# A vision-transformer tower on one core: two programs joined, weights split later, another order around the attention heads, and one exponential per tile

## The chip, the core and the metric

The kernel runs on one core of a Trainium2 chip. Five engines work side by side and meet through semaphores: TensorE (PE, matmuls; PEld is its weight load), VectorE (DVE), ScalarE (ACT), GpSimd (POOL) and SyncE (SP), which issues most transfers. Each engine takes its instructions in the order in which they are written. The metric is the time of one execution on the device in microseconds (us), lower is better; the profile is one execution, read by the hardware profiler.

## The reference, cut to what matters

64 images are cut into 36 patches each, embedded, and given two more tokens: 64 x 38 = 2432 tokens of 256 channels. Then comes an attention block (an mLSTM with four heads of 128 channels) and a feed-forward block with one shared expert and 32 routed ones, of which each token takes the best.

```python
h = embed(x) + positions                         # 64 x 38 tokens of 256
x_mlstm, z = split(layernorm(h) @ W_up)          # 2 x 512 channels
x_act = silu(causal_conv(x_mlstm, 4 taps))
q, k, v = headwise(x_act, Wq), headwise(x_act, Wk), headwise(x_mlstm, Wv)
ig, fg = concat(q, k, v) @ W_ig + b_ig, concat(q, k, v) @ W_fg + b_fg
logD = cumsum(log_sigmoid(fg))[s] - cumsum(log_sigmoid(fg))[t] + ig[t]     # for t <= s
mD = max over t of logD;  Dmat = exp(logD - mD)
C = q @ k.T * 128 ** -0.5 * Dmat
o = (C / max(|sum C|, exp(-mD))) @ v             # per image and head
state = (norm(o) * norm_w + skip * x_act) * silu(z)
h = h + state @ W_down
x2 = layernorm(h);  e = argmax(x2 @ gate_w);  s = sigmoid(max(x2 @ gate_w))
h = h + swiglu_shared(x2) + swiglu_e(x2 * s)     # expert e of 32, I = 512
```

## The kernel before, in words

The work has two parts, each a block of its own with one program per engine; at the end of the first block all engines meet before the second begins. `groups_phase` takes the images in eight groups of eight (304 tokens, four tiles of two images, 76 rows each). It is a software pipeline of eleven steps, written out by hand: `pipeline` calls `step(e, f, a, m)` on each engine, where `e` is the group that is embedded in this step, `f` the one before it (layer norm, up projection, convolution), `a` the one before that (attention), and `m` the oldest (feed-forward: router and shared expert). In five steps all four are there; the last step but two has no `e`, the last but one has only `a` and `m`, the last only `m`. The order of the calls in `step` is the order on that engine.

The names that matter: on PE, `decay` puts the exponent of the attention weights of one tile into a bank (a mask of -1e30, then per head a product of `pick` with `top_parts`, the negated running maximum of the gates), `heads` is the product of the weights with the values, `gate_up(m, k)` a quarter of the shared expert's two up products (12 matmuls), `ranks` counts tokens per expert, `shared_down` is the shared expert's second layer, `heads_t`, `down` and `att_rows` close the attention. On ACT, `decay(a, j)` takes the exponential of each of the four heads apart, since each has its own bias, a column of `a_gate`. On DVE, `weigh(a, j)` multiplies it with the scores, `expert_act(m, k)` multiplies the two halves of `gate_up(m, k)`, `rank_of` works on the counts, `head_stats`, `head_var`, `norm_2`, `last_channel` and `head_norm` normalise the heads. The banks of the heads are `ab` (2 to 5), those of the projections `fb` (0, 1), those of the feed-forward `mb` (6, 7).

Weights are kept in two parts (`_hi`, `_lo`), so that three fast products make one of nearly full precision. For the shared expert ACT and DVE split them (`split_shared`) in step 1, behind the first group's `f`; the last write of this preparation is `put_gate_columns`, and PE's first `q_of` waits for it (25 marks on `s_prep`).

`experts_phase` takes 32 slots of 128 tokens, one per expert, and up to 18 more for experts with more tokens. A slot: `x_of` (transposes), two `gate_up`, transposes of the product, `down`. Weights come in four buffers ahead. The rows of a slot were scattered by POOL in `xs_put` and `base_put` at the end of each group's `m`; `late_rows` finds the rows of tokens past 128, `count_slots` the extra slots. SP loads the first slot's rows when all 32 scatters (`s_x_put`) have landed.

Of the kernel before, what the change touches and what calls it, by code (L numbers as in the profile page):

```python
# [45 lines left out]
def groups_phase(nc, patches, w_lin, pos, cols, w_up, conv, chan, wq, wk, wv, wvt, w_gates, b_gates,  # L46
# [6 lines left out]
    with ExitStack() as ctx:  # L53
# [6 lines left out]

        ident = sort.ident
# [7 lines left out]
        up_hi = sb("up_hi", [128, KD, 2 * INNER], f32r)  # L69
        up_lo = sb("up_lo", [128, KD, 2 * INNER], f32r)  # L70
# [16 lines left out]
        pick = sb("pick", [AT, NT * NH, R], f32r)  # L87
# [11 lines left out]
        xn = sb("xn", [R, NT, D])  # L99
        xn_hi = sb("xn_hi", [128, KD, GT], f32r)  # L100
        xn_lo = sb("xn_lo", [128, KD, GT], f32r)
        xm = sb("xm", [128, 2, KI, GS, S])
        raw_vg = sb("raw_vg", [128, KI, GT])
        silu_z = sort.silu_z
        y = sb("y", [128, KI, GS, S])
        raw_qk = sb("raw_qk", [128, KI, GT])
        x_act = sort.x_act
        q_t = sb("q_t", [128, NH, NT, QW])
        c_t = sb("c_t", [R, NT, NH, QW])
        v = sb("v", [R, NT, INNER])  # L110
# [10 lines left out]
        top_parts = sb("top_parts", [AT, R], f32r)  # L121
        cw = sb("cw", [R, NT, NH, R])
# [103 lines left out]
        s_parts = sem("s_parts")  # L226
        s_top_mm = sem("s_top_mm")
# [64 lines left out]
        PREP_ALL = 25  # L292
# [18 lines left out]
        with nc.Block() as block:  # L311

            @block.sync
            def _(sp):
                sp.dma_start(lin_w[:], w_lin).then_inc(s_w_emb, 16)
# [7 lines left out]
                for dst, src in [(pos_t, pos), (col_t, cols)]:  # L323
                    sp.dma_start(dst[:], src).then_inc(s_w_emb, 16)
# [31 lines left out]
            def _(pool):  # L356
# [1599 lines left out]
```

## Time and profile before

| | |
|---|---|
| median of three runs | 744.8 us (743.41 to 746.59) |
| the profiled execution | 744.39 us |
| its span, first to last instruction | 742.6 us, mean granted PE clock 0.931 |
| PE busy | 657.5 us, 89% |
| DVE, ACT, POOL busy | 469.3, 390.6, 227.6 us |
| in the chain that ended last | PE 26%, issue 1%, DVE 1%, others 0% |

The profiled execution is 1.8 us longer than its span, and 0.4 us shorter than the median. The chain of waits reaches back only through the experts' part, so it says nothing of the groups; those are read from the timeline by engine. In a timeline row the first number is the start in us from the span's start, the second the time from the first start to the last end of the row's instructions, then engine, line and operation, and in brackets how long the engine sat idle before it and who ended that. Matmuls overlap, so the next row may begin before the row's end.

### The profile page before, as it was taken

The numbers are of one execution on the slowest core, as the hardware profiler recorded it, in microseconds if no ns is written. First come the engines' busy times: TensorE is split into PE (matmuls) and PEld (weight loads), VectorE is DVE, ScalarE is ACT, GpSimd is POOL, SyncE is SP. The second block draws the span as 40 slices with busy tenths as digits, with TensorE's granted clock in tenths as the row PEclk, the third lists the DMA queues.
The fourth block names the chain that finished last, engine by engine and source line by source line (L and its number), as shares of the span: only waits on it lengthen the run. The fifth ranks groups of instructions, "written<-read, shape, count | busy, mean of one in ns | idle before, by whom it ended". The sixth has DMA issues, their size and how long they took to land. (4 is left out here: it accounts for less than half of the span.)

```text
span 742.6 us, 11751 instructions
## 1 busy us (share of the span) xinstructions
PE 657.5 (89%) x4013; PEld 556.0 (75%) x4013; DVE 469.3 (63%) x1529; ACT 390.6 (53%) x856; POOL 227.6 (31%) x249
## 2 busy tenths in 40 slices
PE   4868999899999999899899978858599999999992
PEld 3757878878878878878878857737388888888782
DVE  1543666766766766766766763654567676767660
ACT  1335729629629629629629528302366666666660
POOL 3000011133033033133133133243356664312541
PEclk9698689999999999999999997977799999999997
DMA  8149010020020020020010010042599999999860
GB/s 307 64 124 359 24 49 1 18 83 18 18 82 19 18 82 19 18 81 19 19 33 20 18 32 16 18 137 102 174 369 379 378 380 375 322 409 345 292 241 15
DMA packets 46261, 101.69 MB, mean 137 GB/s; under 512 B 10952, under 2 KB 32246, under 8 KB 41329
## 3 DMA queue, kind: packets, MB, share of 16 engines
q1 hardware_dynamic: 35184, 89.07, 33.1%
q0 software_dynamic: 9488, 8.52, 4.4%
q10 hardware_dynamic: 1520, 3.23, 1.3%
q8 instruction: 37, 0.61, 0.3%
q14 instruction: 32, 0.25, 0.1%
HBM read 80.17 MB, written 23.32 MB: 139 GB/s over the span
## 5 line engine op out<-in xcount | busy, mean ns | idle before, releaser
L407 POOL TENSOR_TENSOR rstd_h<-var_h,minus_half 76x4 f32<-76x4 f32 x32 | 32.3, 1010 | 223.2 <-DVE var_h L844 223.2
L1671 POOL DMA_INDIRECT out<-rows,bg x32 | 37.5, 1171 | 72.0 <-DVE rows L1741 65.2
L1843 PE MATMUL bank<-w_hi,x_hi 128*128 128x512 f32 x148 | 57.6, 471 | 1.9 <-DVE x_lo L1753 1.9
L1075 PE MATMUL bank<-patch,lin_w 128*128 128x288 f32 x192 | 51.9, 424 | 7.8 <-DMA col_t<-cols 7.8
L451 ACT ACTIVATE att_t<-bank 128x304 f32<-128x304 f32 x16 | 6.8, 423 | 88.0 <-PE bank L1226 87.3
L1075 PEld LDWEIGHTS bank<-patch,lin_w 128*128 128x128 f32 x192 | 37.6, 200 | 18.2 <-POOL v L384 7.8
L748 DVE SCALAR_TENSOR_TENSOR y<-xm,conv_t,y 128x296 f32<-128x296 f32 (+2 forms) x96 | 44.3, 512 | 10.7 <-ACT xm L451 10.7
L1843 PE MATMUL bank<-w_lo,x_hi 128*128 128x512 f32 x148 | 47.0, 399 | 0.0
L1843 PE MATMUL bank<-w_hi,x_lo 128*128 128x512 f32 x148 | 46.6, 396 | 0.0
L1747 DVE TENSOR_TENSOR w_lo<-wts,w_hi 128x1024 fp32r<-128x1024 f32 x36 | 43.1, 1217 | 0.2 <-ACT w_hi L1794 0.2
L1466 POOL DMA_INDIRECT x_zone_dram<-xs_rows,spot x32 | 37.6, 1175 | 16.1 <-issue 8.9
L1466 POOL DMA_INDIRECT b_zone_dram<-base_rows,spot x32 | 37.1, 1160 | 16.5 <-issue 16.5
L1774 DVE TENSOR_TENSOR act_e<-silu_e,bank 128x512 f32<-128x512 f32 x37 | 25.5, 688 | 26.3 <-PE bank L1843 22.5
L1107 PE MATMUL bank<-xn_hi,up_hi 128*128 128x304 f32 x128 | 35.8, 364 | 5.6 <-DVE xn_lo L734 4.4
L1226 PE MATMUL bank<-hst,down_w 128*128 128x304 f32 x128 | 37.3, 448 | 3.5 <-DVE hst L864 3.5
L1107 PE MATMUL bank<-xn_hi,sgu_hi 128*128 128x304 f32 x128 | 33.5, 346 | 7.4 <-DVE logits L928 3.7
L1664 POOL DMA_INDIRECT listed_dram<-token,late_spot x32 | 36.3, 1134 | 9.8 <-issue 9.8
L1794 ACT ACTIVATE w_hi<-wts 128x1024 fp32r<-128x1024 f32 x36 | 37.0, 1050 | 1.9 <-DMA wts<-w_exp 1.9
L1818 ACT ACTIVATE silu_e<-bank 128x512 f32<-128x512 f32 x37 | 22.1, 596 | 28.8 <-PE bank L1843 28.0
L1741 DVE SCALAR_TENSOR_TENSOR rows<-bank,bg 128x256 f32<-128x256 f32 x37 | 15.7, 425 | 33.6 <-PE bank L1860 19.1
L1226 PEld LDWEIGHTS bank<-hst,down_w 128*128 128x128 f32 x128 | 26.1, 205 | 12.9 <-DVE hst L867 3.7
L1207 PE MATMUL bank<-v,cw 76*76 76x128 f32 x256 | 34.7, 296 | 1.0 <-DVE cw L798 1.0
(251 smaller groups left out, 1790.9 us busy)
## 6 DMA issues: line engine op xcount, KB each, us to landing
wts<-w_exp SPq DMA_DIRECT2D x18, 1024.0 KB
x_act<-w_exp SPq DMA_DIRECT2D x10, 1024.0 KB
silu_z<-w_exp SPq DMA_DIRECT2D x9, 1024.0 KB
wts_down<-w_exp SPq DMA_DIRECT2D x18, 512.0 KB
patch<-patches SPq DMA_DIRECT2D x8, 864.0 KB, 6.5
down_w<-w_exp SPq DMA_DIRECT2D x10, 512.0 KB
lin_w<-w_exp SPq DMA_DIRECT2D x9, 512.0 KB
b_zone_dram<-act_t SPq DMA_DIRECT2D x1, 4160.0 KB, 28.5
```

What stands on the lines that cost most here:

```text
L407: pool.tensor_tensor(rstd_h[:, j, :], var_h[:, j, :], minus_half[:], ALU.pow).then_inc(s_rstdh, 1)
L748: dve.scalar_tensor_tensor(y[:, k, :, lag:], xm[:, f.p, k, :, 0:S - lag], w, y[:, k, :, lag:], ALU.mult, ALU.add).then_inc(s_conv, 1)
L1075: last = pe.matmul(fb[c][:, 0:GS * N], lin_w[:, k, c * 128:(c + 1) * 128], patch[:, k, :], start=(k == 0), stop=(k == KF - 1))
L1107: last = pe.matmul(dst, weights[w][:, c, at:at + 128], x[part][:, c, :], start=(n == 0), stop=(n == 3 * KD - 1))
L1207: last = pe.matmul(ab[j][0:R, h * 128:(h + 1) * 128], cw[:, j, h, :], v[:, j, h * 128:(h + 1) * 128], start=True, stop=True)
L1226: last = pe.matmul(ab[c][:, 0:GT], down_w[:, k, c * 128:(c + 1) * 128], hst[:, k, :], start=(k == 0), stop=(k == KI - 1))
L1466: pool.indirect_dma_start(zone, bass.IndirectOffsetOnAxis(ap=self.spot[:, t:t + 1], axis=0), rows, None, bounds_check=E * SLOT - 1, oob_is ...
L1664: pool.indirect_dma_start(dram.listed, bass.IndirectOffsetOnAxis(ap=sort.late_spot[:, t:t + 1], axis=0), sort.token[:, t:t + 1], None, bou ...
L1671: pool.indirect_dma_start(out, bass.IndirectOffsetOnAxis(ap=rows_at, axis=0), rows[:, k % 4, :], None, bounds_check=T - 1, oob_is_err=Fals ...
L1747: dve.tensor_tensor(w_lo[:, k % 2, u, :], wts[k % 4][:, u * KD * I:(u + 1) * KD * I], w_hi[:, k % 2, u, :].bitcast(f32), ALU.subtract).the ...
L1794: act.activation(w_hi[:, k % 2, u, :], wts[k % 4][:, u * KD * I:(u + 1) * KD * I], ACT.Copy).then_inc(s_w_hi, 1)
L1843: last = pe.matmul(banks[2 + 2 * e + u][:, :], x[:, e, c * SLOT:(c + 1) * SLOT], w[:, e, u, c * I:(c + 1) * I], start=(n == 0), stop=(n == ...
```

## The change

The two blocks become one: the engines do not meet between the parts, and each walks from its last group into the experts. The last step of the pipeline is taken out of ACT's and DVE's `step` and written as `last_group`, called from the experts' first turn, with the first three splits of expert weights between its calls. SP's last stores are woven into the first loads of the experts' part. `late_rows` moves behind the second expert's product, and the experts use other banks. The shared weights have a buffer of their own and are split one step later; `put_gate_columns` goes into `merge_weights`, and `centre_values` before the embedding. On PE the last two `heads` come before `gate_up(m, 1)`, `up(f, 5)` goes between the heads, `up(f, 6)` before `ranks`, and the first of the four `q_of` products before `att_rows`. The gates no longer enter as ACT's bias: DVE makes `gate_parts`, PE adds them to the bank by one more product per tile, and ACT takes one exponential of 304 columns per tile.

The diff, without the change of indentation of both functions, cut to its core:

```diff
 (groups_phase, ACT)
 def decay(a, j):
 act.wait_ge(s_b_mm, NT * a.n + j + 1)
-for h in range(NH):
-g = NH * j + h
-act.activation(cw[:, j, h, :], ab[j][0:R, h * R:(h + 1) * R], ACT.Exp,
-bias=a_gate[:, g:g + 1]).then_inc(s_dmat, 1)
+act.activation(cw[:, j].rearrange("p h t -> p (h t)"), ab[j][0:R, 0:GT],
+ACT.Exp).then_inc(s_dmat, 1)
...
-if f and f.n == 0: split_shared()
+if f and f.n == 1: split_shared()
...
+def last_group(split):
+m = Group(G - 1, (G - 1) % 2)
+split(0, 0)
+xn2_t_of(m)
+split(0, 1)
+tanh_score(m)
+silu_g_of(m, 0)
+silu_g_of(m, 1)
+score_rows(m)
+silu_g_of(m, 2)
+split(1, 0)
+silu_g_of(m, 3)
+ffn_t_of(m)
 (groups_phase, DVE: merge_weights)
+dve.tensor_copy(q_t[:, :, :, R:], gx_w[:].unsqueeze(2).broadcast_to([128, NH, NT, 2 * NH])
+).then_inc(s_prep, 1)
 (top_gates)
+dve.tensor_scalar(gate_parts[:], ab[0][0:AT, 0:R], -1.0, None, ALU.mult).then_inc(s_gate_parts, 1)
...
+dve.wait_ge(s_gate_parts, 2 * a.n + 1)
+dve.scalar_tensor_tensor(gate_parts[LOW:, :], ab[0][LOW:AT, 0:R], -1.0,
+gate_parts[LOW:, :].bitcast(f32), ALU.mult,
+ALU.subtract).then_inc(s_gate_parts, 1)
 (step)
 weigh(a, 0)
 weigh(a, 1)
+weigh(a, 2)
+weigh(a, 3)
 if m:
 expert_act(m, 0)
 score_of(m)
-if a:
-weigh(a, 2)
-weigh(a, 3)
...
+def last_group(split):
+m = Group(G - 1, (G - 1) % 2)
+ln2_stats(m)
+xn2_of(m)
+split(0, 0)
+xn2_lo_of(m)
+route(m)
+choose(m)
+expert_act(m, 0)
+score_of(m)
+expert_act(m, 1)
+rank_of(m)
+split(0, 1)
+expert_act(m, 2)
+split(1, 0)
+expert_act(m, 3)
+dve.wait_ge(s_past, G)
+sort.count_slots(dve)
+base_of(m)
+sort.table_of(dve)
 (groups_phase, PE: decay)
 for h in range(NH):
-last = pe.matmul(ab[j][0:R, h * R:(h + 1) * R], pick[:, NH * j + h, :], top_parts[:],
-start=False, stop=(h == NH - 1))
+pe.matmul(ab[j][0:R, h * R:(h + 1) * R], pick[:, NH * j + h, :], top_parts[:],
+start=False, stop=False)
+last = pe.matmul(ab[j][0:R, 0:GT], gate_parts[:], pick[:, NH * j:NH * j + NH, :],
+start=False, stop=True)
 (step)
 heads(a, 0)
 heads(a, 1)
+if f: up(f, 5)
+if a:
+heads(a, 2)
+heads(a, 3)
+if m: gate_up(m, 1)
+if f:
+if f.n > 0: mixed_gates(f)
+up(f, 6)
 if m:
-gate_up(m, 1)
 ranks(m)
 gate_up(m, 2)
...
-if a:
-heads(a, 2)
-heads(a, 3)
-if f: up(f, 5)
 if m: gate_up(m, 3)
-if f:
-if f.n > 0: mixed_gates(f)
-up(f, 6)
-up(f, 7)
+if f: up(f, 7)
...
-if a:
-down(a)
-att_rows(a)
+if a: down(a)
+if f: q_of(f, range(0, 1))
+if a: att_rows(a)
 (experts_phase, SP)
+sort.last_rows(0)
+load_gate_up(2, sort.load, 2)
+sort.last_rows(1)
 sp.wait_ge(sort.s_x_put, 16 * TILES)
 load_x(0)
 load_x(1)
 (experts_phase, DVE: turn)
 if k == 0:
-w_lo_of(0, 0)
+sort.last_dve(w_lo_of)
 x_lo_of(k)
...
+if k == 1:
+sort.late_rows(dve)
```

PE in a full step, from the first heads to the counts. `v,cw` is `heads`, `xn2_hi,sgu_hi` and the two like it `gate_up`, `xn_hi,up_hi` and the two like it `up`, `hot` and `past` belong to `ranks`. Before:

```order
L1207 MATMUL bank2<-v,cw 76x128 x4
L1207 MATMUL bank3<-v,cw 76x128 x4
L1107 MATMUL bank6<-xn2_hi,sgu_hi 128x304 x2
L1107 MATMUL bank6<-xn2_hi,sgu_lo 128x304 x2
L1107 MATMUL bank6<-xn2_lo,sgu_hi 128x304 x2
L1107 MATMUL bank7<-xn2_hi,sgu_hi 128x304 x2
L1107 MATMUL bank7<-xn2_hi,sgu_lo 128x304 x2
L1107 MATMUL bank7<-xn2_lo,sgu_hi 128x304 x2
L1258 MATMUL bank7<-hot,before 76x128
```

In the changed kernel, from the same place:

```order
L1259 MATMUL bank2<-v,cw 76x128 x4
L1259 MATMUL bank3<-v,cw 76x128 x4
L1154 MATMUL bank1<-xn_hi,up_hi 128x304 x2
L1154 MATMUL bank1<-xn_hi,up_lo 128x304 x2
L1154 MATMUL bank1<-xn_lo,up_hi 128x304 x2
L1259 MATMUL bank4<-v,cw 76x128 x4
L1259 MATMUL bank5<-v,cw 76x128 x4
L1154 MATMUL bank6<-xn2_hi,sgu_hi 128x304 x2
L1154 MATMUL bank6<-xn2_hi,sgu_lo 128x304 x2
L1154 MATMUL bank6<-xn2_lo,sgu_hi 128x304 x2
L1154 MATMUL bank7<-xn2_hi,sgu_hi 128x304 x2
L1154 MATMUL bank7<-xn2_hi,sgu_lo 128x304 x2
```

The heads of the last two tiles and `up(f, 5)` (bank 1) now stand ahead of `gate_up(m, 1)` (banks 6 and 7); the counts stand further down, behind the gates' products and `up(f, 6)`.

DVE in the same step, from `weigh` (`cw`) to the first row of `rank_of` (`logits<-bank,hot`); `act_t` is `expert_act`, `y` the convolution. Before:

```order
L798 TENSOR_TENSOR cw<-c_t,cw 76x304 x2
L943 TENSOR_TENSOR act_t<-silu_g,bank 128x304
L921 TENSOR_SCALAR score<-tanh_s 76x4
L798 TENSOR_TENSOR cw<-c_t,cw 76x304 x2
L748 SCALAR_TENSOR_TENSOR y<-xm,conv_t,y 128x8x36 x2
L943 TENSOR_TENSOR act_t<-silu_g,bank 128x304
L748 SCALAR_TENSOR_TENSOR y<-xm,conv_t,y 128x8x35 x2
L748 SCALAR_TENSOR_TENSOR y<-xm,conv_t,y 128x8x37 x2
L928 TENSOR_TENSOR logits<-bank,hot 76x128
```

In the changed kernel:

```order
L826 TENSOR_TENSOR cw<-c_t,cw 76x304 x4
L971 TENSOR_TENSOR act_t<-silu_g,bank 128x304
L949 TENSOR_SCALAR score<-tanh_s 76x4
L771 SCALAR_TENSOR_TENSOR y<-xm,conv_t,y 128x8x36 x2
L971 TENSOR_TENSOR act_t<-silu_g,bank 128x304
L771 SCALAR_TENSOR_TENSOR y<-xm,conv_t,y 128x8x35 x2
L771 SCALAR_TENSOR_TENSOR y<-xm,conv_t,y 128x8x37 x2
L956 TENSOR_TENSOR logits<-bank,hot 76x128
```

All four `weigh` come first; between the first and the second `expert_act` one pair of the convolution is left, and everything behind the second stands behind it as before.

DVE at the seam, where the last group goes over into the experts: `base_rows` is the last group's, `o`, `late_f`, `early` and `late_spot` are `late_rows`, `x_lo` and `act_e` belong to the experts. Before:

```order
L950 TENSOR_TENSOR base_rows<-bank,h 76x2x256 x2
L1509 TENSOR_TENSOR o<-hot,start_row 76x1024
L1511 TENSOR_REDUCE late_f<-o 76x32
L1512 TENSOR_SCALAR early<-rank 76x32
L1513 TENSOR_TENSOR late_f<-late_f,rank 76x32
L1514 TENSOR_TENSOR late_spot<-late_f,early 76x32
L1516 CAST table<-bank 1x18
L1517 CAST table<-end_slot 1x1
L311 UNCONDITIONAL_BRANCH
L1734 UNCONDITIONAL_BRANCH
L1747 TENSOR_TENSOR w_lo<-x_act,w_hi 128x1024
L1753 TENSOR_TENSOR x_lo<-bank,x_hi 128x256
```

In the changed kernel, from the same `base_rows`:

```order
L978 TENSOR_TENSOR base_rows<-bank,h 76x2x256 x2
L1573 CAST table<-bank 1x18
L1574 CAST table<-end_slot 1x1
L1811 TENSOR_TENSOR x_lo<-bank,x_hi 128x256
L1835 TENSOR_TENSOR act_e<-silu_e,bank 128x512
L1811 TENSOR_TENSOR x_lo<-bank,x_hi 128x256
L1805 TENSOR_TENSOR w_lo<-silu_z,w_hi 128x1024
L1805 TENSOR_TENSOR w_lo<-wts,w_hi 128x1024
L1835 TENSOR_TENSOR act_e<-silu_e,bank 128x512
L1563 TENSOR_TENSOR o<-hot,start_row 76x1024
L1565 TENSOR_REDUCE late_f<-o 76x32
L1566 TENSOR_SCALAR early<-rank 76x32
```

`late_rows` has moved from before the first expert's `x_lo` to between the second expert's product and the third expert's `x_lo`.


## Rows read from the trace of the kernel before

**Rows 1.** the page: the granted clock of PE in 40 slices of the span, in tenths

```profile
PEclk9698689999999999999999997977799999999997
```

**Rows 2.** two steps of the loop: busy time by engine, granted clock (from:to, us, engines)

```profile
220.00:275.70 55.70, 52.94 (x373) 45.87 (x373) 39.40 (x163) 32.16 (x83) 16.11 (x17) 0.97 0.13 40
275.70:331.30 55.60, 51.83 (x374) 44.50 (x375) 39.31 (x163) 32.16 (x83) 16.12 (x17) 1.00 0.13 40
```

**Rows 3.** first and last `att_rows` of the full steps (start us, us, engine, line)

```profile
108.60 1.07 PE L1084 MATMUL bank<-ident,att_t 128*76 128x128 f32 x8 [0.51 <-ACT att_t L451]
386.90 1.07 PE L1084 MATMUL bank<-ident,att_t 128*76 128x128 f32 x8 [0.51 <-ACT att_t L451]
```

**Rows 4.** PE in one step, from the end of the decays; last, the step after

```profile
240.78 0.87 PE L1107 MATMUL bank<-xn_hi,up_hi 128*128 128x304 f32 x2
244.84 1.91 PE L1207 MATMUL bank<-v,cw 76*76 76x128 f32 x16
249.15 0.22 PE L1258 MATMUL bank<-hot,before 76*76 76x128 bf16 x1 [0.72 <-DVE act_t L943]
251.06 0.52 PE L1107 MATMUL bank<-xn_hi,sgu_hi 128*128 128x304 f32 x2 [0.61 <-DVE logits L928]
251.98 1.91 PE L1207 MATMUL bank<-v,cw 76*76 76x128 f32 x16
259.05 4.25 PE L1285 MATMUL bank<-act_t,sd_w 128*128 128x304 f32 x16
302.01 0.55 PE L1107 MATMUL bank<-xn_hi,sgu_hi 128*128 128x304 f32 x2 [1.03 <-ACT silu_g L580]
```

**Rows 5.** DVE in the same step: the experts' products and the last head channel

```profile
248.53 0.47 DVE L943 TENSOR_TENSOR act_t<-silu_g,bank 128x304 f32<-128x304 f32 x1
252.25 0.47 DVE L943 TENSOR_TENSOR act_t<-silu_g,bank 128x304 f32<-128x304 f32 x1
256.94 0.47 DVE L943 TENSOR_TENSOR act_t<-silu_g,bank 128x304 f32<-128x304 f32 x1
265.13 0.15 DVE L849 SCALAR_TENSOR_TENSOR o<-mv_h,rstd_h 76x4 f32<-76x4 f32 x1
```

**Rows 6.** ACT in the same step: the score copies and the 16 exponentials

```profile
224.79 2.19 ACT L451 ACTIVATE c_t<-bank 76x336 f32<-76x336 f32 x4
240.89 3.49 ACT L541 ACTIVATE cw<-bank,a_gate 76x76 f32<-76x76 f32 x16
```

**Rows 7.** PE in the step without an embedding, after waits

```profile
432.36 1.24 PE L1217 MATMUL bank<-ident,o 76*128 76x76 f32 x16 [0.54 <-DVE o L849]
435.36 5.92 PE L1226 MATMUL bank<-hst,down_w 128*128 128x304 f32 x16 [1.75 <-DVE hst L864]
```

**Rows 8.** PE and DVE at the end of the first group's preparation

```profile
57.00 4.39 PE L1133 MATMUL bank<-x_act,score_w 128*128 128x304 f32 x8 [5.52 <-DVE q_t L704]
54.10 1.22 DVE L661 TENSOR_TENSOR sgu_lo<-hst,sgu_hi 128x1024 fp32r<-128x1024 f32 x1
```

**Rows 9.** the seam: links of the chain of waits (start us, us, what)

```profile
526.55 2.02 DMA xg<-x_zone_dram
535.18 0.69 DVE act_e L1774
539.98 1.73 PE bank L1860 x8
```

**Rows 10.** the seam: PE's last transposes of the groups, first expert product

```profile
521.03 1.07 PE L1084 MATMUL bank<-ident,ffn_t 128*76 128x128 f32 x8 [0.29 <-ACT ffn_t L451]
530.23 1.22 PE L1843 MATMUL bank<-w_hi,x_hi 128*128 128x512 f32 x2 [0.93 <-DVE x_lo L1753]
```

**Rows 11.** the seam: the two long operations of `late_rows` on DVE

```profile
523.00 1.21 DVE L1509 TENSOR_TENSOR o<-hot,start_row 76x1024 f32<-76x1024 bf16 x1
524.25 1.22 DVE L1511 TENSOR_REDUCE late_f<-o 76x32 f32<-76x1024 f32 x1
```

**Rows 12.** the seam: POOL's last scatter of expert inputs

```profile
518.82 1.13 POOL L1466 DMA_INDIRECT x_zone_dram<-xs_rows,spot  x1 [0.30 <-issue]
```

More of the change, by code:

```diff
@@ L226, in groups_phase @@
         s_parts = sem("s_parts")
+        s_gate_parts = sem("s_gate_parts")
         s_top_mm = sem("s_top_mm")
@@ L1266, in gate_up @@
-                def gate_up(m, k):
-                    if k == 0:
-                        pe.wait_ge(s_lgt, m.n + 1)
-                        if m.n == 0:
-                            pe.wait_ge(s_prep, 23)
-                    else:
-                        pe.wait_ge(s_sg, KI * m.n + k)
-                    for u in range(2):
-                        if u and k:
-                            pe.wait_ge(s_act, KI * m.n + k)
-                        if u and k == 2:
-                            pe.wait_ge(s_own, m.n + 1)
-                        at = u * I + k * 128
-                        split_product(mb[u][:, 0:GT], (sgu_hi, sgu_lo), (xn2_hi, xn2_lo), at).then_inc(s_gu_mm, 1)
@@ L1281, in shared_down @@
-                def shared_down(m):
-                    pe.wait_ge(s_act, KI * m.n + KI)
-                    for c in range(KD):
-                        for k in range(KI):
-                            last = pe.matmul(mb[c][:, 0:GT], sd_w[:, k, c * 128:(c + 1) * 128], act_t[:, k, :],
-                                             start=(k == 0), stop=(k == KI - 1))
-                        last.then_inc(s_sd_mm, 1)
-                def ffn_rows(m):
-                    pe.wait_ge(s_ffn, KD * m.n + KD)
-                    to_rows(mb, ffn_t, s_ft_mm)
@@ L1357, in _, with shared_down @@
-                pipeline(pe, step)
+                else:
+                    pe.wait_ge(s_sg, KI * m.n + k)
+                for u in range(2):
+                    if u and k:
+                        pe.wait_ge(s_act, KI * m.n + k)
+                    if u and k == 2:
+                        pe.wait_ge(s_own, m.n + 1)
+                    at = u * I + k * 128
+                    split_product(mb[u][:, 0:GT], (sgu_hi, sgu_lo), (xn2_hi, xn2_lo), at).then_inc(s_gu_mm, 1)
+            def shared_down(m):
+                pe.wait_ge(s_act, KI * m.n + KI)
+                for c in range(KD):
+                    for k in range(KI):
+                        last = pe.matmul(mb[c][:, 0:GT], sd_w[:, k, c * 128:(c + 1) * 128], act_t[:, k, :],
+                                         start=(k == 0), stop=(k == KI - 1))
+                    last.then_inc(s_sd_mm, 1)
@@ L1360 @@
+            pipeline(pe, step)
 class Sort:
```

2226 lines of the change are left out of this document (1129 added, 1097 removed).

## The prediction

> **What bounds the kernel now.** I read the page first. PE is busy for 657.5 of 742.6 us, but with a mean clock of 0.931, and its clock slices [rows 1] stand at 9 in the loop: short stretches of half clock are strewn through it. The chain of waits reaches only through the experts' part, where PE follows itself; the change leaves an expert's work as it is, so that part keeps its length, and the chain only serves at the seam [rows 9].
>
> Second, the windows by step [rows 2]. A full step takes 55.7 us, PE is busy for 52 to 53 of them, DVE for 39.4, ACT for 32.2. So PE bounds the loop, with 3 to 4 us of small waits. The first and last `att_rows` of the five full steps are 108.60 and 386.90 [rows 3]: 278.3 us, 55.66 each. What a reader should see there: each step is the same, whatever is won or lost in one counts five times.
>
> Third, the timeline of PE in one step [rows 4], with DVE's and ACT's beside it [rows 5, 6]. PE's waits are 0.51 for `att_t` [rows 3], 0.72 for the first `act_t` before the counts, 0.61 for DVE to read the counts (`logits`), and, in the step after, 1.03 for `silu_g` between the heads and `gate_up(m, 1)`. In the step shown that last wait is missing, and in its place the 18 products from 240.78 to 244.84 took 4.06 us: at full clock six take 0.92 (251.06 to 251.98), 0.153 each, so 18 take 2.75. The half clock cost 1.3 us there and was free, since `silu_g` would have been waited for anyway: both steps last 55.6 to 55.7, at a granted clock of 0.97 and 1.00 [rows 2]. DVE's stretch between the experts' products is what I rest most on: from 248.53 (`expert_act(m, 1)`) to 256.94 (`expert_act(m, 3)`) DVE has 8.41 us of work in one piece.
>
> **The decay.** PE gets one more product per tile, 304 columns wide, about 0.15 by the price above: 4 x 0.15 = +0.6 per step, on the path. ACT trades 16 exponentials in 3.49 us for four of 304 columns. The nearest rows are the copies of 336 columns, four in 2.19 [rows 6], 0.55 each: 2.0 to 2.2 in all, 1.4 less. ACT waits for PE there, so this only lets the heads start early enough. DVE gets a negation of 48 rows and a small subtraction, 0.2 to 0.4 us, in a stretch where it waits. If that cover were missing, +0.4 per step.
>
> **The order around the heads.** The waits of 0.72, 0.61 and 1.03 all go, because other work stands in each place. But `gate_up(m, 1)` now ends later. The decays end at 240.78 + 0.6 = 241.4; then 36 products (`up(f, 4)`, `gate_up(m, 0)`, `up(f, 5)`, `gate_up(m, 1)`) take 36 x 0.153 = 5.5, and two pairs of heads 2 x 1.7 = 3.4 (244.84 to 246.5, less than the 1.91 of the row since the next row overlaps). End 250.3, where DVE began `expert_act(m, 1)` at 248.53. What stands behind it on DVE is unchanged, so `expert_act(m, 3)` starts 8.41 later at about 258.8 and ends at 259.25. `shared_down` needs it: 259.25 against 259.05 [rows 4]. I take +0.2 per step, +1.0 for five (bounds -0.5 per step, if the copies and products overlap better, and +0.6).
>
> So the small waits become one. PE is through with `up(f, 7)` at 250.3 + 1.05 (gates) + 0.9 + 0.2 (counts) + 1.8 + 1.8 + 0.9, about 257, and then waits about 2.2 us. Behind `shared_down` stand the embedding, `heads_t` and `down`; the last head channel, 265.13 on DVE [rows 5], comes out at about 267, just when PE gets there. No further loss by that (0 to +0.5).
>
> **The clock after that wait.** In the trace, the wait of 1.75 us before `down` was followed by 16 products in 5.92 us [rows 7], and the 5.52 us before `q_of` by eight in 4.39 [rows 8]: half clock, 1.2 GHz. The wait of 1.03 was not: its first pair took 0.55 [rows 4]. The 16 of `shared_down` took 4.25 at full clock, 2.4 GHz. A wait of 2.2 us lies beyond the one of 1.75, so I take half clock: 5.92 - 4.25 = 1.67 per step, 5 x 1.67 = +8.3 (bounds 0 and 5 x 3). And the half clock behind the decays, so far free, is on the path once `silu_g` is not waited for: 1.3 in two of five steps, +2.6 (bounds 0 and 6.5).
>
> For the clock the Trainium skill, "TensorE: Matmul & The Clock Gate", section "HAM oscillation — how this bites in real kernels", speaks for a better outcome: the idle gap that it calls harmful is longer than the one forecast here. By it the +8.3 would not come. The 5.92 us of [rows 7] behind a wait of 1.75 speaks against it, though other waits stood close before that one. This is the second case below.
>
> **`q_of(0)` before `att_rows`.** It fills the 0.51 for `att_t`, but then `q_of(2)` and `q_of(3)` meet the residual of DVE that much earlier: 0 (bounds -0.5 and 0 per step, in the -0.5 above).
>
> **The start.** The first `q_of` waits 5.52 us for `q_t`, whose columns were written behind the split of the shared weights (`sgu_lo` until 55.3) [rows 8]. Now they are written in `merge_weights`: -5.5, up to 2 more if the clock stays up. The split moves a step later: ACT's and DVE's pieces now stand beside a step with attention: +1.0 (0 to 2.7). In the second step the shorter exponentials come before `weigh`: -0.8 (0 to -1.5).
>
> **The steps at the end of the loop.** In the step without an embedding PE waits for `o` directly, 0.54 [rows 7], so the 1.9 by which DVE is later shows: +1.8 (0.5 to 2.5). The step of `a` and `m` alone: +0.9 (0 to 2).
>
> **The seam.** Before, the last scatter of expert rows is issued at 518.82 for 1.13 us [rows 12], PE ends its transposes at 522.1 [rows 10], the load of the first rows takes 2.02 from 526.55 [rows 9], and the first product starts at 530.23. Now no meeting of the engines stands between: scatter landed about 2 us after 520.5 (the last group's `shared_down` is late by the splits that stand between the calls of `last_group`, about 1.8), load 2.0, transposes and `x_lo` about 1.5: 526.1, -4.1. But `late_rows`, two operations of 1.2 us [rows 11] and small ones, 3.1 in all, now stands before the third expert's `x_lo`. PE has about 0.6 us of slack there, so it stalls for 2.5. Net -1.6 (bounds -6.3, where the row loads are not late and `late_rows` is hidden, and +1).
>
> **Sum** against the profiled execution, 744.4 (0.4 below the median of 744.8): -5.5 + 1.0 - 0.8 + 1.0 + 1.8 + 0.9 - 1.6 = -3.2, then +8.3 + 2.6 = +10.9; together +7.7, 752.1. I forecast 752.
>
> **The rivals.**
> First, the gap keeps the clock. Everything else as above: 744.4 - 3.2 = 741.2, with its own spread of 3. For it: at 1.03 us the clock stood, and the projections before the gap are dense work at full clock. Against it: 1.75 was followed by 5.92. It decides at the `shared_down` of each step: 4.25 or about 5.9. This is the case on the other side. Chance 0.30.
>
> Second, the seam opens fully on top of that: the expert rows have landed when the last group's shared product ends, first expert product near 523.9 instead of 526.1, -6.3 in place of -1.6: 736.5. For it: the scatters are issued by 520 [rows 12]; against it: they wait for positions that DVE counts after its own split, and `late_rows` of 2.4 us in two rows [rows 11] must stand somewhere. Chance 0.17.
>
> Third, PE loses the clock for longer: DVE's continuous stretch also delays `heads_t`, so that a second wait follows the first while the clock is at half: 3 us per step in place of the 1.67, 5 x 1.3 more, 759 and above. For it: `o` ends only at about 267. Chance 0.05.
>
> The forecast has the remaining 0.48, with its own range of 746 to 760.
>
> **Chances and range.** 0.5% is 3.7 us, about what a measurement of this kernel can tell from no change: faster is below 741.1, slower above 748.5. Faster: half of the first rival 0.15, the second 0.17, and 0.02 of others, 0.34. No change: the other half of the first 0.15 and the low end of the forecast 0.05, 0.20. Slower: the rest, 0.46. The range reaches to 735, to take in most of the second rival, and to 761.
>
> **What the profile of the changed kernel would show.** The first `q_of` near 51.5 with no wait. In every full step an idle time of about 2.2 us on PE before `shared_down`, ended by DVE's `act_t`, and its 16 products in about 5.9 us; with 4.25 the first rival holds. `att_rows` to `att_rows` about 58, or 55.9 by that rival. No wait for `silu_g` or `logits` between the heads and `up(f, 7)`. ACT's exponentials as four near 0.5 us. The first expert product near 526 and a stall of 2.5 us on PE before the third expert's products, ended by DVE. I am wrong in the main term if DVE's stretch between the second and the fourth `expert_act` is shorter than 8.4 us or starts earlier than the sum says, and so the wait isn't there.

## The result and the profile after

| | before | changed |
|---|---|---|
| median | 744.2 us | 759.8 us (759.28 to 760.21, four runs) |
| profiled execution, its span | 744.39, 742.6 us | 759.47, 757.7 us |
| mean granted clock of PE | 0.931 | 0.924 |
| PE busy | 657.5 us | 673.0 us |

The ratio is 1.020, 95% interval 1.018 to 1.023: slower by 15.6 us (whether by more than 2% the interval leaves open), inside the stated range, 7.8 above the forecast of 752. In the ratios of this document, runs more than 1.5% above the fastest of their kernel are left out (six of e9's eleven, one of e12's six). Five full steps first. The first and the last `att_rows` of the changed kernel's full steps:

```profile
100.79 1.04 PE L1131 MATMUL bank<-ident,att_t 128*76 128x128 f32 x8
394.69 1.04 PE L1131 MATMUL bank<-ident,att_t 128*76 128x128 f32 x8
```

The loop is reached 7.8 us earlier than before [rows 3], and its five steps take 293.9 us, 15.6 more. Two of them as windows, columns as in [rows 2]:

```profile
217.19:275.29 58.10, 54.07 (x378) 46.13 (x377) 39.79 (x165) 30.11 (x71) 16.00 (x17) 0.97 0.13 39
335.09:394.69 59.60, 55.59 (x378) 47.30 (x377) 39.85 (x165) 30.22 (x71) 15.98 (x17) 0.94 0.08 22
```

All five full steps now have stretches of half clock (granted 0.97, 0.97, 0.97, 0.94, 0.94); before, two had (0.97 and 0.97, the others 1.00). PE in the first of the two, and `shared_down` of the step after:

```profile
238.55 0.55 PE L1154 MATMUL bank<-xn_hi,up_hi 128*128 128x304 f32 x2
239.57 0.71 PE L1154 MATMUL bank<-xn_hi,sgu_hi 128*128 128x304 f32 x2
242.61 2.00 PE L1259 MATMUL bank<-v,cw 76*76 76x128 f32 x16
246.95 0.52 PE L1154 MATMUL bank<-xn_hi,sgu_hi 128*128 128x304 f32 x2
250.89 0.22 PE L1312 MATMUL bank<-hot,before 76*76 76x128 bf16 x1
258.35 4.36 PE L1339 MATMUL bank<-act_t,sd_w 128*128 128x304 f32 x16 [2.64 <-DVE act_t L971]
...
316.48 6.05 PE L1339 MATMUL bank<-act_t,sd_w 128*128 128x304 f32 x16 [2.63 <-DVE act_t L971]
```

The waits for `silu_g`, `act_t` and `logits` [rows 4] are gone, and one of 2.6 us stands in their place before `shared_down`. The 18 products from 238.55 to 242.61 take 4.06 us, half clock again for most of them, and nothing behind them hides it. In the last full step (the second window) the half clock behind the decays lasts twice as long, from 355.4 to 362.3; in the fourth it came a second time, at `shared_down` (316.48). DVE in the same step, the last three products of the shared expert, and the last channel of the heads:

```profile
248.97 0.47 DVE L971 TENSOR_TENSOR act_t<-silu_g,bank 128x304 f32<-128x304 f32 x1 [4.65 <-PE bank L1154]
253.13 0.47 DVE L971 TENSOR_TENSOR act_t<-silu_g,bank 128x304 f32<-128x304 f32 x1
257.82 0.47 DVE L971 TENSOR_TENSOR act_t<-silu_g,bank 128x304 f32<-128x304 f32 x1
266.02 0.15 DVE L877 SCALAR_TENSOR_TENSOR o<-mv_h,rstd_h 76x4 f32<-76x4 f32 x1
```

DVE waits 4.65 us for PE and starts `expert_act(m, 1)` 31.78 us behind `att_rows`, where it was 28.53 [rows 3, 5]: 3.25 later. From there to `expert_act(m, 3)` are 8.85 us (8.41 before). ACT's four exponentials and, for the size, its score copies:

```profile
221.94 2.19 ACT L463 ACTIVATE c_t<-bank 76x336 f32<-76x336 f32 x4
237.97 1.35 ACT L549 ACTIVATE cw<-bank 76x304 f32<-76x304 f32 x4
```

1.35 us instead of 3.49 [rows 6]. The start: `q_of` no longer waits [rows 8].

```profile
50.45 3.25 PE L1180 MATMUL bank<-x_act,score_w 128*128 128x304 f32 x8
```

The step without an embedding [rows 7]; PE waits for `o` 2.02 us where it waited 0.54:

```profile
443.79 1.92 PE L1269 MATMUL bank<-ident,o 76*128 76x76 f32 x16 [2.02 <-DVE o L877]
447.46 6.08 PE L1280 MATMUL bank<-hst,down_w 128*128 128x304 f32 x16 [1.75 <-DVE hst L892]
```

The seam [rows 9 to 12], POOL, then PE, then DVE (`late_rows`):

```profile
535.43 1.13 POOL L1520 DMA_INDIRECT x_zone_dram<-xs_rows,spot  x1 [0.30 <-issue]
```

```profile
538.21 1.07 PE L1131 MATMUL bank<-ident,ffn_t 128*76 128x128 f32 x8 [0.29 <-ACT ffn_t L463]
540.75 0.44 PE L1898 MATMUL bank<-ident,xg 128*128 128x128 f32 x2 [1.47 <-DMA xg<-x_zone_dram]
542.12 0.72 PE L1909 MATMUL bank<-w_hi,x_hi 128*128 128x512 f32 x2 [0.93 <-DVE x_lo L1811]
555.63 0.73 PE L1909 MATMUL bank<-w_hi,x_hi 128*128 128x512 f32 x2 [2.27 <-DVE x_lo L1811]
```

```profile
552.12 1.22 DVE L1563 TENSOR_TENSOR o<-hot,start_row 76x1024 f32<-76x1024 bf16 x1
553.37 1.22 DVE L1565 TENSOR_REDUCE late_f<-o 76x32 f32<-76x1024 f32 x1
```

From the last `att_rows` (508.36) to the first expert product are 33.8 us; before, 37.2 (493.08 to 530.23). From there to the end 215.6 against 212.4.

The account of the 15.1 us between the two spans: -7.8 before the loop; +15.6 in five full steps; +4.6 and +2.9 in the two steps behind them; -3.4 to the first expert product; +3.2 from there.

### The profile page after: what moved, and what is told of

It is laid out like the page before. It is cut to its first block, busy times and chain, and to the rows that moved or that the text cites. A ratio compares the mean times of both kernels' runs of the same rounds, so it can differ in the third digit from the quotient of the medians.

```text
span 757.7 us, 11735 instructions
## 1 busy us (share of the span) xinstructions
PE 673.0 (89%) x4045; PEld 564.9 (75%) x4045; DVE 471.7 (62%) x1545; ACT 374.0 (49%) x760; POOL 232.9 (31%) x249
## 4 chain that ended last, share of the span: by engine, by line
PE 77%; DVE 12%; issue 3%; ACT 3%; DMA 2%; POOL 1%; SPq 0%; DVEq 0%; POOLq 0%
PE bank L1154 15%; PE bank L1909 14%; PE bank L1928 8%; PE bank L1122 6%; PE bank L1280 5%; PE bank L1259 4%; PE bank L1339 3%; PE bank L1917 2%; PE bank L1218 2%; PE bank L1180 2%; PE bank L1131 2%; PE bank L1250 2%; DVE h L901 1%; PE bank L1247 1%; DVE stats_h L858 1%
## 5 line engine op out<-in xcount | busy, mean ns | idle before, releaser
L1909 PE MATMUL bank<-w_hi,x_hi 128*128 128x512 f32 x148 | 57.6, 471 | 4.2 <-DVE x_lo L1811 4.2
L1729 POOL DMA_INDIRECT out<-rows,bg x32 | 39.3, 1227 | 60.5 <-DVE rows L1799 48.4
L1339 PE MATMUL bank<-act_t,sd_w 128*128 128x304 f32 x128 | 36.6, 441 | 18.3 <-DVE act_t L971 18.3
L971 DVE TENSOR_TENSOR act_t<-silu_g,bank 128x304 f32<-128x304 f32 x32 | 15.1, 471 | 57.8 <-PE bank L1154 56.7
L1122 PEld LDWEIGHTS bank<-patch,lin_w 128*128 128x128 f32 x192 | 37.0, 197 | 17.8 <-POOL v L396 7.8
L1339 PEld LDWEIGHTS bank<-act_t,sd_w 128*128 128x128 f32 x128 | 24.7, 197 | 28.4 <-DVE act_t L971 20.3
L1722 POOL DMA_INDIRECT listed_dram<-token,late_spot x32 | 38.7, 1210 | 19.5 <-DVE late_spot L1568 10.1
L588 ACT ACTIVATE silu_g<-bank 128x304 f32<-128x304 f32 x32 | 13.5, 420 | 61.6 <-PE bank L1154 61.6
```

What stands on the lines that cost most here:

```text
L1122: last = pe.matmul(fb[c][:, 0:GS * N], lin_w[:, k, c * 128:(c + 1) * 128], patch[:, k, :], start=(k == 0), stop=(k == KF - 1))
L1339: last = pe.matmul(mb[c][:, 0:GT], sd_w[:, k, c * 128:(c + 1) * 128], act_t[:, k, :], start=(k == 0), stop=(k == KI - 1))
L1722: pool.indirect_dma_start(dram.listed, bass.IndirectOffsetOnAxis(ap=sort.late_spot[:, t:t + 1], axis=0), sort.token[:, t:t + 1], None, bou ...
L1729: pool.indirect_dma_start(out, bass.IndirectOffsetOnAxis(ap=rows_at, axis=0), rows[:, k % 4, :], None, bounds_check=T - 1, oob_is_err=Fals ...
L1909: last = pe.matmul(banks[2 + 2 * e + u][:, :], x[:, e, c * SLOT:(c + 1) * SLOT], w[:, e, u, c * I:(c + 1) * I], start=(n == 0), stop=(n == ...
```

## Experiments

Medians are of the runs of each kernel; "before" ran on the same chip each time (743.97 to 745.23 us). Steps are read as the distance of two `att_rows`. Where runs of one kernel are spread, the mean granted clock mostly goes with them, so it is given for the profiled execution. Clock and steps are of that one execution, and it isn't always a typical one: it is the fastest of its kernel in e6 (737.0 us), e10 (754.3), e11 (741.0) and e12 (751.4), the slowest in e5 (739.5), and 757.8 in e9.

| kernel | median | ratio to before, interval | clock | the five full steps |
|---|---|---|---|---|
| before | 744.2 | | 0.931 | 55.6 to 55.8 |
| changed | 759.8 | 1.020 (1.018 to 1.023) | 0.924 | 58.1 to 59.8 |
| e1 old order | 748.0 | 1.006 (1.003 to 1.008) | 0.926 | 56.7, four of 58.0 |
| e2 old decay | 752.7 | 1.011 (1.007 to 1.015) | 0.925 | 57.6 to 58.8 |
| e3 both old | 741.5 | 0.994 (0.992 to 0.996) | 0.928 | 55.7 to 56.0, one 57.3 |
| e4 | 768.7 | 1.031 (1.025 to 1.037) | 0.926 | 57.9 to 60.8 |
| e5 | 737.4 | 0.989 (0.986 to 0.993) | 0.942 | 55.1 (three), 56.7, 58.5 |
| e6 | 743.3 | 0.997 (0.995 to 0.999) | 0.939 | 55.7 to 55.9, one 57.6 |
| e7 | 749.9 | 1.008 (1.004 to 1.011) | 0.934 | 55.9, 56.1, three of 57.4 |
| e8 | 744.3 | 0.999 (0.995 to 1.003) | 0.934 | 55.6 to 56.1, one 59.0 |
| e9 | 746.7 (five runs), 758.7 (six) | 1.001 (0.998 to 1.004), of the five | 0.918 | 58.0 to 58.1 |
| e10 | 759.3 | 1.020 (1.017 to 1.024) | 0.937 | 58.2 (three), 59.8, 60.1 |
| e11 | 743.0 | 1.000 (0.997 to 1.003) | 0.935 | 55.0, 55.0, 56.5, 56.7, 58.0 |
| e12 | 760.5 | 1.022 (1.018 to 1.027) | 0.921 | 55.2 to 61.4 |

The eleven runs of e9 fall into two groups, five of 744.5 to 747.6 us (clock 0.930 to 0.934) and six of 757.1 to 759.9 (0.915 to 0.918); the profile is of the second.

### e1: the old order

```diff
 heads(a, 0)
 heads(a, 1)
-if f: up(f, 5)
-if a:
-heads(a, 2)
-heads(a, 3)
 if m: gate_up(m, 1)
-if f:
-if f.n > 0: mixed_gates(f)
-up(f, 6)
 if m:
 ranks(m)
 gate_up(m, 2)
+if a:
+heads(a, 2)
+heads(a, 3)
+if f: up(f, 5)
...
```

> The changed kernel with PE's and DVE's order around the heads put back as it was before; the gates' product, the start, the seam and the early first q_of stay. Theory 1 (the new order sets expert_act(m, 1) 3.25 us later within the step, DVE's 8.4 to 8.9 us of work behind it are in one piece, so shared_down starts 2.1 us later; and the half clock behind the decays, that the wait for silu_g hid before, is now paid): the wait of 2.63 us before shared_down is gone, the five full steps last 55.5 to 56.3 us instead of 58.8, and the kernel takes 739 to 746 us, 14 to 20 less than the 759.8 of the changed kernel. Rival (the decay product itself makes the steps longer, by PE's 0.63 us and the clock): steps stay at 57 or above, 751 or more.

The diff shows PE; on DVE `weigh(a, 2)` and `weigh(a, 3)` go back behind `score_of(m)`. 748.0 us: 11.8 less than the changed kernel, between the two expected ranges (2 above the one, 3 below the other). The wait before `shared_down` is gone (first row: the mask of the last decay, then the heads, the counts, `shared_down`):

```profile
233.71 0.47 PE L1248 MATMUL bank<-mask_bf,ident_bf 76*76 76x304 bf16 x1
239.81 1.95 PE L1260 MATMUL bank<-v,cw 76*76 76x128 f32 x16
244.15 0.22 PE L1313 MATMUL bank<-hot,before 76*76 76x128 bf16 x1 [0.73 <-DVE act_t L971]
254.03 4.25 PE L1340 MATMUL bank<-act_t,sd_w 128*128 128x304 f32 x16
```

So the wait was the order's. But four of five steps stay at 58.0, since half clock now begins within the decays (0.47 for a mask that takes 0.32 at full clock, as the row of e5 below shows) and lasts up to the heads. The first theory holds for the wait, the rival for the length of the steps.

### e2: the old decay

```diff
-act.activation(cw[:, j].rearrange("p h t -> p (h t)"), ab[j][0:R, 0:GT], ACT.Exp)
+for h in range(NH):
+act.activation(cw[:, j, h, :], ab[j][0:R, h * R:(h + 1) * R], ACT.Exp, bias=a_gate[:, g:g + 1])
...
-last = pe.matmul(ab[j][0:R, 0:GT], gate_parts[:], pick[:, NH * j:NH * j + NH, :],
-start=False, stop=True)
```

> The changed kernel with the decay as it was before: no gates' product on PE, 16 exponentials with a bias per step on ACT; the new order stays. Theory 1: the wait before shared_down stays at about 2.6, the step loses the 0.63 us of the gates' product and, if the half clock behind the decays goes with it, 1.4 more: steps of 56.7 to 58.1 us, 745 to 756 us. Rival (the decay makes the steps longer): steps near 55.7, about 743. A second rival: without the shorter exponentials the heads of the last two tiles are late in the new order, and the steps get longer than 58.1.

752.7 us. `shared_down` of two steps, one after the other:

```profile
257.82 4.36 PE L1333 MATMUL bank<-act_t,sd_w 128*128 128x304 f32 x16 [2.63 <-DVE act_t L968]
313.68 6.05 PE L1333 MATMUL bank<-act_t,sd_w 128*128 128x304 f32 x16 [2.63 <-DVE act_t L968]
```

The wait of 2.63 is the same in both, the clock behind it is not. Four of the five steps of this kernel have it at half clock (6.05), and in those four the stretch behind the decays was at full clock; the one with 4.36 had half clock there, and took 58.8. The sequence that the forecast rests on, wait and then half clock, exists, then: in four of five steps here, in one of five in the changed kernel.

These four steps also say what the order costs by itself. `shared_down` starts 38.9 to 39.1 us behind `att_rows` in them, as before the change (38.9 to 39.1), although PE now waits 2.6 us in one piece ahead of it. The order alone delays nothing there; the step is 1.9 us longer, and 1.7 of that is `shared_down` at half clock. In the changed kernel it starts at 41.16: the gates' products (0.65) and the half clock behind the decays (1.4) come on top, and DVE, with hardly a wait from `expert_act(m, 1)` on, passes both on.

### e3: both old

> The changed kernel with both put back, order and decay; what is left of the change is the joined programs, the start, late_rows behind the second expert and the first q_of before att_rows. Theory 1: steps as before, 55.7 us; what is left gives 7.8 us at the start and 0 to 1 net at the seam (first expert product 3.4 earlier within the last group, then a stall): 735 to 738 us. Rival (joining the programs costs in the loop too): 742 or more.

741.5 us, 3.6 less than before, between the two expected ranges: joining, start and seam are a gain, less than the 7.8 and 3.4 us of the changed kernel's trace, since this one's loop begins only at 103.35 (5.3 earlier than before) and one of its steps took 57.3. The order alone is then worth 11.2 us (e2 - e3), the decay alone 6.6 (e1 - e3), together 17.8; measured for both, on another chip, 18.3. They add up. Neither is the price of instructions alone: with the new decay at full clock a step takes 55.1 us (e5 below), less than the 55.7 of e3's shortest, so what the decay costs in e1 is the half clock in its steps.

### e4: `expert_act(m, 3)` early

```diff
+if m: expert_act(m, 3)
 if a:
 norm_2(a, 0)
 head_stats(a, 0)
 head_var(a, 0)
-if m: expert_act(m, 3)
```

> The changed kernel with expert_act(m, 3) put ahead of norm_2 and the first head_stats on DVE, so that shared_down need not wait for them (2.7 us of work). Theory A (DVE's whole chain from expert_act(m, 1) to the last head channel bounds the step, not the product alone): the wait of 2.63 before shared_down goes to under 0.5, but PE then waits about as long before heads_t, ended by DVE's o; steps change by less than 0.5 us, 757 to 761 us. Theory B (the wait before shared_down is the whole cost): steps shorter by 2.2 to 2.6, about 747 us.

768.7 us, 9 more than the changed kernel, which neither theory gave. In each step three waits came in place of the one:

```profile
260.42 4.36 PE L1338 MATMUL bank<-act_t,sd_w 128*128 128x304 f32 x16 [1.31 <-DVE act_t L971]
265.80 3.15 PE L1121 MATMUL bank<-patch,lin_w 128*128 128x288 f32 x12 [1.02 <-ACT silu_z L502]
270.96 1.25 PE L1268 MATMUL bank<-ident,o 76*128 76x76 f32 x16 [1.14 <-DVE o L877]
```

3.5 us together instead of 2.6. That the wait moves to `heads_t` and is not saved was theory A's point, and it is shown: DVE's chain to the last channel is what PE runs into. The length was wrong, because DVE itself now waited 1.18 us for `silu_g` in front of `expert_act(m, 3)`, with the heads' statistics queued behind it. This accounts for the five full steps, which take 4.5 us more than in the changed kernel (298.4 us). The two steps behind them take 6.8 more (120.4 against 113.7); there PE waits 3.06 and 2.76 us for `ffn_t`.

### e5: `up(f, 4)` ahead of the decays, with the old order

```diff
 if m: route(m)
+if f: up(f, 4)
 if a:
 tops_t(a)
 decay(a, 0)
...
 decay(a, 3)
-if f: up(f, 4)
```

> The kernel of e1 (old order, new decay) with one edit: up(f, 4), six dense products of 304 columns, stands between the router's products and the decays instead of behind the decays. In e1 PE waited for nothing there, and yet four of five steps had the decays and what follows at half clock (masks to heads 8.8 us, 6.6 at best expected). Theory (a stretch of small products costs the clock: router, masks, decays, which the gates' product made longer): with dense work in the middle the clock stays at 2.4 GHz, masks to heads falls by 0.9 for the moved product and 1.5 to 2.2 for the clock, steps of 55.8 to 56.4 us, 738 to 742 us. Rival (the fall has nothing to do with that stretch, or the heads then wait for DVE's cw): steps stay near 58, 747 or more.

737.4 us, the fastest kernel measured here, 1.1% (0.7 to 1.4) faster than before. A mask at full clock, and two windows:

```profile
236.66 0.32 PE L1248 MATMUL bank<-mask_bf,ident_bf 76*76 76x304 bf16 x1
```

```profile
215.20:270.29 55.09, 52.36 (x379) 44.59 (x377) 39.58 (x165) 30.26 (x71) 16.10 (x17) 1.00 0.13 40
327.00:382.09 55.09, 52.37 (x379) 44.60 (x377) 39.59 (x165) 30.26 (x71) 15.95 (x17) 1.00 0.09 25
```

Here the new decay does what it can: steps of 55.09, 0.57 shorter than before, with a product more and at full clock. The expected reason, dense work in the middle of small products, looked confirmed. But its own trace has two steps of 58.5 and 56.7, with half clock at the end of the decays or behind them in both (from 125.91 and from 293.16), and in the first another stretch at 112.3, after a wait of 1.21 us for `xn`, in the step in which DVE now splits the shared weights (the steps behind it wait 0.34 there). Its five full steps together take 280.5 us, more than the 278.3 before; what this execution gains lies at the start (the loop is reached 7.0 us earlier) and at the seam. The next runs took the reason back.

### e6 and e8: `late_rows` in three pieces, and all together

```diff
+if 1 <= k <= 3:
+sort.late_rows(dve, k)
 dve.wait_ge(s_se, k + 1)
...
-if k == 1:
-sort.late_rows(dve)
```

> The kernel of e3 (order and decay of before) with late_rows of 3.1 us not in one piece behind the second expert's product but in three pieces, one in each of the second to fourth turn, ahead of DVE's expert product. Theory (the stall of 2.27 us before the third expert's products is late_rows and counts in full, with half clock behind it): stall under 0.3, 2.3 to 4 us less than e3's 741.5: 737.5 to 739. Rival (the stall is hidden by a later wait for weights): 741 to 742.

> What the other runs point to, together: joined programs and new start, order and decay of before, no early first q_of, up(f, 4) ahead of the decays, late_rows in three pieces. Theory: steps of 55.6 to 55.9 us all through and no stall at the third expert, 732 to 737 us. Rival (with 16 exponentials the heads now wait for cw, since up(f, 4) no longer covers them): a wait of 0.5 to 1 per step before the heads, 738 to 742.

e6 743.3, e8 744.3 us: no gain over e3's 741.5, and both above either expected range. In e6 the stall of 2.27 us is gone, and two others came:

```profile
544.96 0.73 PE L1912 MATMUL bank<-w_hi,x_hi 128*128 128x512 f32 x2 [0.65 <-DVE w_lo L1808]
567.46 0.73 PE L1912 MATMUL bank<-w_hi,x_hi 128*128 128x512 f32 x2 [0.82 <-DVE w_lo L1808]
```

From the first expert product to the end are 213.3 us, in e3 213.7. Of the 2.27 us that the stall gave, the two waits for the split weights took back 1.5; a gap of 0.91 us at 696.70, for which the profile names no cause and which e3's trace doesn't have, took most of the rest. That is the rival in kind, a later wait for weights. The wait for `cw` before the heads, which e8's rival expected, is not in its trace. e8 shows further that `up(f, 4)` ahead of the decays does not keep the clock: one of its steps took 59.0, with half clock from the fourth mask on.

### e7: the wait filled

```diff
+if e: embed(e, 0)
 if m: shared_down(m)
-if e: embed(e, 0)
```

> The kernel of e2 (new order, old decay) with embed(e, 0) ahead of shared_down on PE, and silu_z(f, 2) ahead of silu_g(m, 3) on ACT so that it can start there: the wait of 2.6 us before shared_down is filled with 2.9 us of dense products. In e2 shared_down to heads_t took 9.67 us behind that wait where 7.98 is full clock. Theory A (the wait costs the clock): no wait over 0.5 there, shared_down at full clock, steps near 56 us, 743 to 746 us. Theory B (DVE's chain to the last head channel bounds the step, the wait only moves): PE waits 1 to 2.5 us before heads_t for o and runs down at half clock, steps of 57 to 58.5, 751 to 756.

749.9 us, between the theories. PE does not idle 2.6 us in one piece any more:

```profile
255.32 3.15 PE L1119 MATMUL bank<-patch,lin_w 128*128 128x288 f32 x12 [0.99 <-ACT silu_z L502]
258.31 4.26 PE L1333 MATMUL bank<-act_t,sd_w 128*128 128x304 f32 x16
264.92 1.24 PE L1263 MATMUL bank<-ident,o 76*128 76x76 f32 x16 [0.78 <-DVE o L874]
```

With 0.52 for `ffn_t` it waits 2.3 us in three pieces. `shared_down` is at full clock in every full step, which speaks for the wait as what cost the clock in e2. But behind the decays four of e2's five steps were at full clock, and only two are here; the steps with half clock there take 57.4, the others 55.9 and 56.1. The fall moved; it was not avoided.

### e9 and e10: the same edit elsewhere

e9 is the kernel of before with the new decay and `up(f, 4)` first; a buffer of the start was cut to the size in use to make room for `gate_parts`. e10 is the changed kernel with `up(f, 4)` first.

> The kernel of before, with its two blocks, its start, its order around the heads and its seam, and two edits: the new decay (one exponential per tile, gates' product on PE) and up(f, 4) ahead of the decays. It separates the loop's share of e5's gain from the start's and the seam's. Theory (the pair is worth 0.5 us a step, since the wait of 1.03 for silu_g goes and 0.63 of products come; the joined programs and the start are worth the rest): steps of 55.1 us, 740 to 743 us. Rival (all of e5's gain is the pair): 737 to 738; other rival (the pair gives nothing without the joined programs): 745.

> The changed kernel with up(f, 4) ahead of the decays and nothing else; the new order around the heads stays. Theory (one fall of the clock per step, at whichever weak stretch comes first: with the decays in dense company it comes behind the wait before shared_down, as in e2): masks to heads short by 2.2 us, wait before shared_down still over 1.8 us, its products at half clock in most steps, steps near 57.5 us, 750 to 755 us. Rival (the decay stretch alone costs the clock): shared_down to heads_t stays at 7.98, steps of 56.2 to 56.8, 745 to 749. Either way more than e5's 737.4, by the 2 us or so per step that the new order costs.

e9 takes about 746.7 us or about 758.7 us with the same instructions. A window of the second kind, and the masks in it:

```profile
221.79:279.81 58.02, 55.34 (x377) 47.30 (x377) 39.57 (x165) 30.32 (x71) 16.00 (x17) 0.94 0.13 39
```

```profile
242.50 0.32 PE L1203 MATMUL bank<-mask_bf,ident_bf 76*76 76x304 bf16 x1
243.65 0.47 PE L1203 MATMUL bank<-mask_bf,ident_bf 76*76 76x304 bf16 x1
```

PE was busy 55.34 us for what took 52.36 in e5's window, at 0.94 against 1.00: 2.9 us per step are the clock and nothing else, and the fall sits between the third and the fourth mask although the dense products stand right before. This execution is one of the longer ones; e5's trace above and e11's below show the same fall in kernels with the same edit. By the five shorter runs the pair of edits gives nothing on the kernel of before (1.001), nearest to the rival of 745. e10: 759.3, as the changed kernel and above both expected ranges, wait of 2.63 in each step, `shared_down` at half clock in one of five. Neither theory: full clock in the decays did not move the fall to `shared_down`; it came right behind them.

### e11 and e12: the early `q_of`, and an even denser mix

e11 is e5 with all four `q_of` behind `att_rows`; e12 is e1 with the six products of `up(f, 4)` spread, two behind each of the first three decays.

> The kernel of e5 without the early first q_of: all four behind att_rows, as before. Theory of the prediction (the early product fills a wait of 0.5 us and opens one of 0.43 behind it): no difference, 736 to 739 us, wait of 0.51 for att_t back. Rival (it is a gain of 0.5 us in each of five steps): 740 to 741.

> The kernel of e1 (old order, new decay) with the six dense products of up(f, 4) spread between the four decays, two behind each of the first three. In e9, e10 and e11 half clock came at or behind the decays although up(f, 4) stood ahead of them, so the theory of e5 as it stood has fallen. Theory that is left (a stretch of small products invites the fall, and only a denser mix avoids it): masks to heads near 6.0 us in all steps, steps of 55.1 us, 733 to 738 us with a spread under 4. Rival (the fall comes at its own time, set by what the steps before did; moving dense work by a few us only shifts which product it hits): some steps of 56.5 to 58.0 again, runs spread over 5 us or more, median 738 to 748.

e11: 743.0 us, but with clocks of 0.924 to 0.936 where e5 had 0.939 to 0.946. At full clock its steps are 54.96 and 54.99, e5's 55.09 to 55.12: the early product is worth nothing, -0.1. The 743.0 lies above both expected ranges, and the difference to e5 is the clock's: one step took 58.0, with the fall between the third and the fourth mask:

```profile
343.36 0.47 PE L1248 MATMUL bank<-mask_bf,ident_bf 76*76 76x304 bf16 x1
```

e12: 760.5 us, runs of 751.4 (clock 0.921) to 765.9 (0.904): the densest mix is the worst of the kernels with the old order and the new decay. In the profiled execution, the fastest, three steps were 58.2, 58.2 and 61.4, one 55.2. What was left of the theory has fallen too; the rival fits in kind (runs spread over 14 us), though its 738 to 748 us were too low.

## Why the prediction was right, and where not

It was right in sign, in place and in the biggest new wait; that the number came close is in part luck, since the largest term came to a fifth of its size and others to more than theirs. Step by step:

- **The order around the heads.** Forecast: `expert_act(m, 1)` 1.9 later, `shared_down` behind a wait of 2.2, +0.2 per step. Measured: 3.25 later, wait 2.63, `shared_down` at 41.16 behind `att_rows` where it was 39.05, +2.1. The step that failed is the treatment of the half clock behind the decays: it was entered as 1.3 us in two of five steps, and came in all five, +1.4 each, and 1.5 more in the last (59.60 against 58.10). That is the greater part of the 2.1: by e2's four steps at full clock there (38.95) and the 0.65 of the products, `shared_down` would have started near 39.6, an estimate, inside the forecast's bound of +0.6. The rest is "DVE's work behind it is in one piece": 8.85 instead of 8.41, for DVE's short waits for the counts and for `gate_up(m, 2)`. And 0.28 from `shared_down` to the next `att_rows`.
- **The clock after the wait.** +8.3 was forecast, +1.7 came: one of five `shared_down` took 6.05. e2 shows the sequence, wait and then half clock, in four of five; the step that failed is "a wait of 2.2 us lies beyond the one of 1.75, so I take half clock". For its own place the first rival held. The third, with its 759 us and more, came nearest to the number, but not by its mechanism: in no full step does a second wait stand before `heads_t`. The Trainium skill ("TensorE: Matmul & The Clock Gate", section "HAM oscillation — how this bites in real kernels") leaned that way; the 6.05 behind 2.63 in e2 and here shows that half clock can follow a gap it would let pass, the 4.36 behind the same gap that it need not.
- **The clock in all.** PE was busy for 273.3 us in the five steps, 261.1 before: 12.2 more. The gates' product is 5 x 0.67 = 3.3 (3.26 against 2.58 to 2.63 us for the decays), which leaves about 8.9 for the clock; half of what the half clock grew by (23.9 us now, 6.8 before) gives 8.5, an estimate that fits. PE idles 3.4 more (20.6 against 17.2 us in the five windows). That makes 15.6. The two clock terms were +10.9 in the forecast: nearly the right sum for the wrong reasons, and 6.7 us of waits and products had been put at 1.0.
- **Decay.** PE +0.65 per step against 0.6: right. ACT 1.35 instead of the 2.0 to 2.2 worked out from copies of 336 columns, which take longer each (0.55) than the exponentials (0.34).
- **Start.** -7.8 against -5.5 - 0.8 and up to 2 for the clock: within the bounds. The later split of the shared weights cost 0.2 (first full step, in which it now stands, 58.29, the next two 58.11 and 58.10), not 1.0; in e5 it went with half clock of its own.
- **The two steps behind the loop.** +4.6 and +2.9 against 1.8 and 0.9. `heads_t` waits 2.02 for `o` in both (before, 0.54 in the first and 2.02 in the second), and the wait before `shared_down` is there too, 2.63 and 1.87 (before none and 0.63). PE idles 2.8 and 1.7 us more, and is busy 1.9 and 1.1 more. The forecast put the gates' product and the clock at nothing here, and had no wait before `shared_down`.
- **Seam.** First product -3.4 against -4.1, stall 2.27 against 2.5: right. From the first product to the end +3.2, where 2.5 was counted; half clock from 556.8 to 560.2, behind the stall, goes with it. The second rival fell: the last scatter is still the one that is waited for, issued at 535.43, 27.1 us behind the last `att_rows` (25.7 before), so PE waits 1.47 for `xg`. e6 adds what the forecast did not see: most of what is won by removing the stall comes back as waits for split weights.
- **`q_of(0)`.** Nothing, as forecast (e11).

## What stays open

What makes the clock fall in one run of a step and not in another with the same instructions (e2, e5, e9, e11) isn't settled. Whether the wait before `shared_down` is itself the cause where half clock follows it, or only one of the places for it, is argued from e2 and e7, not shown. Shown is: a full step has mostly one such stretch, at the decays, behind them, or behind the wait before `shared_down` (two in the changed kernel's fourth step and e5's first); putting dense products before or between the decays does not prevent it; and it can repeat step after step, as in e9, where it began 21.1 us behind `att_rows` in all five steps. Why the executions of e9 fall into two groups isn't known; only one of the longer was profiled. Whether e5's 737.4 would hold in many more runs is open for the same reason: e11 differs from it by a product that costs nothing at full clock, and its runs reach 749.5.

## What to carry to other kernels

Small waits that are filled by other work don't add to a gain when the work that fills them delays what another engine, itself without slack from there on, waits for: sum that engine's chain first. And where PE's clock moves between its levels, read the granted clock of every window before crediting a few per cent to an edit; a gain or loss of 1 to 2% here was often the same instructions at another clock.

## What the runs showed of the hardware

- The same program took 744.5 to 759.9 us on one core (e9), at mean granted clocks of 0.934 to 0.915; e12 751.4 to 765.9 at 0.921 to 0.904. About 0.8 us for each 0.001 of clock. In the experts' part, dense products throughout, the windows from 560 to 720 us had full clock (1.00) in before, the changed kernel, e3, e5 and e6.
- The same wait of 2.63 us was followed by 16 products in 4.36 us or in 6.05 us in neighbouring steps (e2).
- One exponential of 76 x 304 takes 0.34 us of ACT's time in a row of four (1.35), four of 76 x 76 with a bias 0.87 (3.49 for 16).
